# Attention and a 60-expert layer on one core: the last chunk's members by one-hot products

## The reference

```python
x = x + attn(layernorm(x))     # 16 query heads, 4 key/value heads of 16, RMS norm on q and k, RoPE, no mask
x = x + ffn(layernorm(x))

def ffn(x):
    shared = (silu(x @ Wg) * (x @ Wu)) @ Wd * sigmoid(x @ w_gate)      # 704 hidden
    probs = softmax(x @ gate_w.T)                                      # 60 experts
    weights, sel = top_k(probs, 4)
    for e in range(60):                                                # each 176 hidden
        acc += cw[:, e] * ((silu(x @ W1[e].T) * (x @ W3[e].T)) @ W2[e].T)
    return shared + acc
```

## Time and profile before

| | us |
|---|---|
| median of 3 runs | 790.94 |
| lowest, highest | 782.4, 792.96 |
| the profiled execution | 785.71 |
| its span, first to last instruction | 783.9 |
| PE busy in the span | 664.1 |
| DVE, ACT, POOL busy | 471.6, 513.3, 390.6 |

### The profile page before, as it was taken

The page is one execution under the profiler, slowest core; times in us unless marked ns, Lnnn a source line. Parts: engine busy times, 40 slices in busy tenths (PEclk is TensorE's granted clock), DMA queues, the critical chain, the costliest instruction groups (busy, mean ns, idle before and its releaser), DMA issues.

```text
span 783.9 us, 17631 instructions
## 1 busy us (share of the span) xinstructions
PE 664.1 (85%) x5559; PEld 333.9 (43%) x5559; DVE 471.6 (60%) x1290; ACT 513.3 (65%) x880; POOL 390.6 (50%) x356
## 2 busy tenths in 40 slices
PE   3578999999999989996979399999989898779900
PEld 1363333343433433455858287444434343334400
DVE  4782434336534454527583325999778797589645
ACT  1559778988898888862232112898778787768800
POOL 2134062164022265446052447788888888778700
PEclk9959999999999999999999699999999999889955
DMA  5000000000004000059100123366667586673178
GB/s 176 0 1 1 1 1 1 1 1 28 1 28 139 28 29 20 9 135 153 17 28 1 10 62 102 95 219 186 222 211 230 183 247 198 182 223 82 71 265 283
DMA packets 43293, 75.89 MB, mean 97 GB/s; under 512 B 8216, under 2 KB 24028, under 8 KB 43204
## 3 DMA queue, kind: packets, MB, share of 16 engines
q1 hardware_dynamic: 33316, 53.81, 23.1%
q0 software_dynamic: 9888, 20.98, 9.2%
HBM read 58.07 MB, written 16.68 MB: 95 GB/s over the span
## 4 chain that ended last, share of the span: by engine, by line
PE 55%; DMA 10%; DVE 9%; POOL 9%; issue 7%; ACT 6%; SPq 1%; ACTq 1%; DVEq 1%; POOLq 0%
PE p_o L1495 15%; PE p_s L1483 10%; PE p_gu L1651 5%; POOL expert_out L772 3%; DMA expert_out<-ys,goes_to 3%; PE p_y L1672 3%; POOL xs L752 3%; DMA members<-place,slot 2%; DMA fin<-expert_out 2%; POOL members L699 2%; ACT placed L791 2%; DMA xs<-x_rows,choice_i 2%; PE p_st L1435 2%; PE bench L1422 2%; PE p_xs L1641 1%
## 5 line engine op out<-in xcount | busy, mean ns | idle before, releaser
L850 ACT ACTIVATE probs<-p_s 128x1024 f32<-128x1024 f32 x256 | 242.4, 1037 | 38.9 <-PE p_s L1483 36.6
L791 ACT ACTIVATE placed<-ring 88x512 f32 x256 | 150.3, 626 | 16.6 <-PE p_d L1593 9.3
L1321 DVE COPY placed<-ring 128x704 f32 x316 | 153.9, 529 | 8.9 <-SPq L578 6.4
L1495 PE MATMUL p_o<-probs,vext 128*32 128x512 f32 x1024 | 136.1, 604 | 0.5 <-DVE enr L1047 0.5
L772 POOL DMA_INDIRECT expert_out<-ys,goes_to x79 | 123.2, 1559 | 26.0 <-issue 18.0
L699 POOL DMA_INDIRECT members<-place,slot x64 | 64.6, 1010 | 142.7 <-PE p_o L1495 100.0
L752 POOL DMA_INDIRECT xs<-x_rows,choice_i x79 | 112.3, 1422 | 39.7 <-issue 19.8
L1651 PE MATMUL p_gu<-placed,xsT 128*32 128x352 f32 x1264 | 114.4, 481 | 0.7 <-DVE placed L1321 0.2
L1483 PE MATMUL p_s<-qst,kst 64*128 64x512 f32 x512 | 95.1, 447 | 2.3 <-ACT probs L850 1.6
L1672 PE MATMUL p_y<-placed,hT 88*32 88x256 f32 x1264 | 85.0, 387 | 7.4 <-ACT hT L791 7.3
L1483 PEld LDWEIGHTS p_s<-qst,kst 64*128 64x128 f32 x512 | 39.0, 184 | 87.1 <-ACT probs L850 76.4
(11 more groups left out here) (237 smaller groups left out, 1047.9 us busy)
## 6 DMA issues: line engine op xcount, KB each, us to landing
ring<-in_w_dram SPq DMA_DIRECT2D x60, 352.0 KB
ring<-in_w_dram SPq DMA_DIRECT2D x60, 176.0 KB
fin<-expert_out SPq DMA_DIRECT2D x16, 512.0 KB, 6.5
x_rows<-rows SPq DMA_DIRECT2D x4, 520.0 KB, 3.6
out_dram<-xres SPq DMA_DIRECT2D x4, 512.0 KB, 6.1
x2T_kept<-xt SPq DMA_DIRECT2D x3, 512.0 KB, 2.9
x2r<-x2T_kept SPq DMA_DIRECT2D x3, 512.0 KB, 8.8
sup<-in_sup_dram SPq DMA_DIRECT2D x2, 704.0 KB, 6.3
```

What stands on the lines that cost most here:

```text
L791: return nc.scalar.activation(o, i_, ACT.Copy, **kw)
L850: nc.scalar.activation(probs[:, j % NPB, :], p_s[j % NSB][:, :], ACT.Exp, scale=SCALE)\
L1321: last = v.tensor_copy(placed13[:, i % N13, h, :], ring[:, bass.ds(ring_at(tile, h), W13)])
L1495: last = mm(p_o[32 * g_:32 * g_ + 32, :], vext[c // 2][:, kb, rr // 2 + KP * h, :], probs[:, (2 * u + half) % NPB, h * QC:(h + 1) * QC], s ...
```

## The change

The last chunk's tokens no longer go through the DRAM table. The scatters of chunks 0 to 2 stay.

- `totals` is cut in two. Its first half (number of blocks of each expert, where its blocks begin) now stands ahead of `rank`; its second, `blocks`, makes block numbers and slots. For this the sum of `mask` and the running total `macc` are made in `route2`, not in `rank`.
- For the last chunk `rank` adds the beginning of the expert's blocks times 32, so the slot is the position in the list of all tiles; shift and mask by 128 give tile and row of each choice (`at_f`).
- `hots` makes on DVE, for each of the 16 choices and groups, a one-hot row over the 79 tiles (`tile_hot`) and one over the 128 rows, times the token's number less `REAL` (`place_hot`). `late` multiplies them on PE, 16 fp32 products summed in one PSUM bank, and `join` adds the sum to `block_members` after its load.
- POOL loads `block_members` when `blocks_ready` and the 48 scatters of chunks 0 to 2 are there.
- The order `after` is new; `down` is two entries, one for each pair of groups; `members` stands 4 gate/ups earlier. `THIRD` is thereby 13, not 17, and the number of gathers ahead of the gate/ups is 40 - 3 x 11 = 7, then 3 behind each of 11 gate/ups, 40 in all.

```diff
+        at_i = low("at_i", [P, 2, TQ * TOPK], i32)
+        at_f = low("at_f", [P, 2, TQ * TOPK])
+        from_none = low("from_none", [P, TQ * TOPK])
...
+        HALF = TQ * TOPK // 2
+        tile_hot = [t.rearrange("p n i -> p (n i)")[:, 0:HALF * NTILE].rearrange("p (n i) -> p n i", i=NTILE)
+                    for t in (rows[:, 0:TQ, :], hot[:, :, :, :].rearrange("p t k e -> p (t k) e"))]
+        place_hot = [t[:, :, :].rearrange("p a c -> p (a c)").rearrange("p (n i) -> p n i", i=P) for t in (enr, enc)]
...
-                 ("gu", 1, 0), ("down", 0, 0),
-                 ("soft", C3, 0), ("gu", 1, 1), ("rank", C3, 0), ("rank2", C3, 0), ("gu", 1, 2), ("totals", 0, 0), ("gu", 1, 3),
-                 ("split", 2, 0), ("gu", 1, 4), ("tables", 0, 0), ("gu", 1, 5), ("gu", 2, 0), ("down", 1, 0),
-                 ("gu", 2, 1), ("gu", 2, 2), ("split", 3, 0), ("gu", 2, 3), ("gu", 2, 4), ("members", 0, 0),
-                 ("gu", 2, 5), ("gu", 3, 0), ("down", 2, 0)]
-        after += [("gu", 3, f) for f in range(1, NFS)] + [("down", 3, 0)]
+                 ("gu", 1, 0), ("soft", C3, 0), ("down", 0, 0), ("totals", 0, 0), ("rank", C3, 0), ("rank2", C3, 0),
+                 ("down", 0, 1), ("gu", 1, 1), ("blocks", 0, 0), ("gu", 1, 2), ("hots", 0, 0), ("gu", 1, 3),
+                 ("split", 2, 0), ("tables", 0, 0), ("gu", 1, 4), ("late", 0, 0), ("gu", 1, 5), ("gu", 2, 0),
+                 ("join", 0, 0), ("down", 1, 0), ("members", 0, 0), ("down", 1, 1), ("gu", 2, 1), ("gu", 2, 2),
+                 ("split", 3, 0), ("gu", 2, 3), ("gu", 2, 4), ("gu", 2, 5), ("gu", 3, 0), ("down", 2, 0),
+                 ("down", 2, 1)]
+        after += [("gu", 3, f) for f in range(1, NFS)] + [("down", 3, 0), ("down", 3, 1)]
...
-            scatter(3, 0, TQ * TOPK)
-
 
             pool.wait_ge(blocks_ready, 1)
-            pool.wait_ge(scattered, 16 * NT * TOPK)
+            pool.wait_ge(scattered, 16 * (NT - TQ) * TOPK)
...
-            gathered = 4
+            gathered = NXS - 3 * (NCH * NFS - THIRD)
...
-
-            def rank(n, c):
-                v.tensor_tensor(hot[:, :, :, :], hot[:, :, :, :],
-                                bench[:, 0:TQ * E].rearrange("p (t o e) -> p t o e", o=1, t=TQ)
-                                .to_broadcast([P, TQ, TOPK, E]), ALU.mult).then_inc(bench_read, 1)
+                dve.wait_ge(mask_ready, c + 1)
                 v.tensor_reduce(mask_sum[:, :], mask[:, :, :].bitcast(fp32).rearrange("p t e -> p e t"), X_AXIS,
                                 ALU.add).then_inc(mask_summed, 1)
                 dve.wait_ge(mask_summed, c + 1)
                 v.tensor_tensor(macc[:, 1 - c % 2, :], macc[:, c % 2, :].bitcast(fp32), mask_sum[:, :], ALU.add)\
                     .then_inc(macc_ready, 1)
...
+            def rank(n, c):
+                ranks = bench[:, 0:TQ * E].rearrange("p (t e) -> p t e", t=TQ)
+                if c == C3:
+
+                    v.scalar_tensor_tensor(out=lg_now[:, :, 0:E], in0=cnt[:, 3:4, :].to_broadcast([P, TQ, E]),
+                                           scalar=float(BLK), in1=ranks, op0=ALU.mult, op1=ALU.add)\
+                        .then_inc(bench_read, 1)
+                    dve.wait_ge(bench_read, n + 1)
+                    v.tensor_tensor(hot[:, :, :, :], hot[:, :, :, :],
+                                    lg_now[:, :, 0:E].unsqueeze(2).to_broadcast([P, TQ, TOPK, E]), ALU.mult)\
+                        .then_inc(ranked, 1)
+                    return
+                v.tensor_tensor(hot[:, :, :, :], hot[:, :, :, :],
+                                ranks.unsqueeze(2).to_broadcast([P, TQ, TOPK, E]), ALU.mult).then_inc(bench_read, 1)
+
...
+                if c == C3:
+                    count(v.tensor_copy(slot[:, at:at + TQ * TOPK], rank_now[:, :, :].rearrange("p t k -> p (t k)")))
+                    v.tensor_single_scalar(at_i[:, 0, :], slot[:, at:at + TQ * TOPK], P.bit_length() - 1,
+                                           ALU.logical_shift_right)
+                    v.tensor_scalar(from_none[:, :], place[:, at:at + TQ * TOPK], -float(REAL), None, ALU.add)
+                    count(v.tensor_single_scalar(at_i[:, 1, :], slot[:, at:at + TQ * TOPK], P - 1, ALU.bitwise_and))
+                    v.tensor_copy(at_f[:, :, :], at_i[:, :, :]).then_inc(at_ready, 1)
...
             def totals():
 
-                def of(n):
-                    return eid[:, n * PER:(n + 1) * PER]
-
-                block_no, passed, real, whose, begins, inside, row_, row_or_none, slots, two, four = map(of, range(11))
                 dve.wait_ge(totals_in_psum, 1)
-                for h in range(PER):
-                    v.tensor_scalar(block_no[:, h:h + 1], tile_i[:, 0:1], float(PER), float(h), ALU.mult, ALU.add)
                 v.memset(cnt[:, 1, :], 1.0)
                 count(v.tensor_scalar(cnt_i[:, 0, :], p_tab[0][:, 0:E], float(BLK - 1), None, ALU.add))
                 count(v.tensor_single_scalar(cnt_i[:, 1, :], cnt_i[:, 0, :], BLK.bit_length() - 1,
                                              ALU.logical_shift_right))
                 count(v.tensor_scalar(cnt[:, 0, :], cnt_i[:, 1, :], 1.0, None, ALU.max))
                 count(v.tensor_tensor_scan(cnt[:, 2, :], cnt[:, 1, :], cnt[:, 0, :], 0.0, ALU.mult, ALU.add))
-                v.tensor_tensor(cnt[:, 3, :], cnt[:, 2, :], cnt[:, 0, :], ALU.subtract)
+                count(v.tensor_tensor(cnt[:, 3, :], cnt[:, 2, :], cnt[:, 0, :], ALU.subtract))
+
+            def blocks():
+
+                def of(n):
+                    return eid[:, n * PER:(n + 1) * PER]
+
+                block_no, passed, real, whose, begins, inside, row_, row_or_none, slots, two, four = map(of, range(11))
+                for h in range(PER):
+                    last = v.tensor_scalar(block_no[:, h:h + 1], tile_i[:, 0:1], float(PER), float(h), ALU.mult, ALU.add)
+                count(last)
...
+            def hots():
+
+                dve.wait_ge(at_ready, 1)
+                dve.wait_ge(rows_stored[C3 - 1], 16)
+                for n, to in enumerate(tile_hot):
+                    v.tensor_tensor(to, iota[:, 0:NTILE].unsqueeze(1).to_broadcast([P, HALF, NTILE]),
+                                    at_f[:, 0, n * HALF:(n + 1) * HALF].unsqueeze(2).to_broadcast([P, HALF, NTILE]),
+                                    ALU.is_equal)
+                for n in range(TQ * TOPK):
+                    last = v.tensor_scalar(place_hot[n // HALF][:, n % HALF, :], iota[:, :], at_f[:, 1, n:n + 1],
+                                           from_none[:, n:n + 1], ALU.is_equal, ALU.mult)
+                last.then_inc(hots_ready, 1)
+
+            def join():
+                dve.wait_ge(members_loaded, 16 * PER)
+                dve.wait_ge(late_in_psum, 1)
+                whole = block_members[0:NTILE, :, :].rearrange("p h r -> p (h r)")
+                v.tensor_tensor(whole, whole, p_tab[1][0:NTILE, 0:P], ALU.add).then_inc(members_joined, 1)
...
-                elif kind == "down" and c < NCH - 1:
-                    for q in range(TQ):
+                elif kind == "down" and (c < NCH - 1 or f):
+                    for q in (2 * f, 2 * f + 1):
...
+                for q in range(2, TQ) if half else ():
+                    pe.wait_ge(shared_added, c * TQ + q - 1)
+                    for f in range(NFS):
+                        last = part(q, f)
+                    last.then_inc(sdown_in_psum, 1)
+                if half:
+                    return
...
+                elif kind == "late":
+                    pe.wait_ge(hots_ready, 1)
+                    pe.wait_ge(bench_read, NJOBS)
+                    for n in range(TQ * TOPK):
+                        last = mm(p_tab[1][0:NTILE, 0:P], tile_hot[n // HALF][:, n % HALF, :],
+                                  place_hot[n // HALF][:, n % HALF, :], start=(n == 0), stop=(n == TQ * TOPK - 1))
+                    last.then_inc(late_in_psum, 1)
                 elif kind == "members":
-                    pe.wait_ge(bench_read, NJOBS)
-                    pe.wait_ge(members_loaded, 16 * PER)
-                    tr(p_tab[1][:, 0:NTILE], block_members[0:NTILE, :, :].rearrange("p h r -> p (h r)"),
+                    pe.wait_ge(members_joined, 1)
+                    pe.wait_ge(tables_ready, 1)
+                    tr(p_tab[0][:, 0:NTILE], block_members[0:NTILE, :, :].rearrange("p h r -> p (h r)"),
                        ident[0:NTILE, 0:NTILE]).then_inc(members_in_psum, 1)
```

More of the change, by code:

```diff
@@ L100, in attention_moe_block @@
         ones = keep("ones", [P, P], f32r)
-        iota_e = keep("iota_e", [P, E])
-        iota_i = keep("iota_i", [P, E], i32)
+        iota = keep("iota", [P, P])
+        iota_i = keep("iota_i", [P, P], i32)
         iota_k = keep("iota_k", [P, TOPK])
@@ L353, in attention_moe_block @@
         rank_ready = sem("rank_ready")
+        ranked = sem("ranked")
         exp_in = sem("exp_in")
@@ L360, in attention_moe_block @@
         totals_in_psum = sem("totals_in_psum")
```

(44 more changed lines are left out.)

18 lines of the change are left out of this document (7 added, 11 removed).

## The result

| | before | changed |
|---|---|---|
| median | 790.94 us | 767.26 us |
| lowest, highest | 782.4, 792.96 | 764.2, 769.28 |
| the profiled execution | 785.71 | 764.2 |
| its span | 783.9 | 762.4 |
| first product of the expert stage | 490.34 | 483.96 |

The ratio is 0.972, 95% interval 0.964 to 0.980: faster, by 23.7 us. Run again in a later group the same two kernels gave 0.985 (0.979 to 0.990), 13.1 us; the experiments come back to this. Of the 21.5 us between the two profiled executions, 6.4 lie ahead of the expert stage and 15.1 in it and its tail.

What follows compares the result with a forecast made beforehand. PE was taken to wait at a 15.4 us standstill and, in the expert stage, on POOL's issue. 785.7 - 11.4 - 12.7 = 761.6; with half of the 5.2 up to the median given back, 764 us, range 748 to 779.

Steps and rivals of the forecast that it cites:

- the stop: Around 440 to 445 us PE, DVE and ACT all stand; claimed to cost 15.4 us in all, slow clock included.
- The walk: Step-by-step timing of the new order from `mask` to ("gu",2,1) at 427.6 us, giving -11.4 us for the shared stage.
- the new steps cost PE 4.0: Shared stage: ("gu",2,1) starts at 427.6 instead of 423.60, so the added work takes 4.0 us of the 15.4 removed.
- The port: At 402 to 407 us, `hots` on DVE locks POOL out: each load 1.24 us later, 5 us in all, sum unchanged.
- The line through two points of the earlier trace: Expert stage: a tile takes (k + 2.03)/1.18 us for k POOL operations; 0.85 us an operation, -12.7 us for 15.
- the waiting for rows: Expert stage: the 9.5 us of waiting for gathered rows were expected gone, counted within the -12.7 us.
- (a): Expert stage bound by transfers, not POOL's issue, so gathers moved ahead gain nothing: 777 us; chance 0.15.
- (c): Expert stage: every gather moved ahead is worth POOL's full period: 748 us; chance 0.10.
- (b): Shared stage: new DVE steps eat the gain from the removed standstill, by clock and late members: 775 us; chance 0.12.
- (d): Three gaps within 10 us leave PE at 1.2 GHz for the rest of the shared stage: 830 us; chance 0.04.
- a gap over 3 us: Sign: no PE gap of more than 3 us was to appear between 400 and 480 us.
- above the 5: Sign: `late` on PE was to take 3.5 to 5 us.

Runs made afterwards that it cites:

- the run in portions: Changed kernel with `hots` and `late` cut into parts with gate/ups between them: 764.16 us beside 765.86 of the changed kernel, ratio to the kernel before 0.981.

## Why the prediction was right, and where it was not

The time was 767.26 for 764.0, inside the range, and the profiled execution took 764.2 for 761.6. The mechanism was the one forecast: the stop is gone, and gathers moved ahead make the expert stage shorter. That the sum is so near is partly luck: the shared stage gave 5.0 us too little and the expert stage 2.4 too much. Point by point:

- **The stop is gone**, as said: the loads waited for the block numbers alone (401.74; predicted 401.8), `join` waited for nothing, and 440 to 445 us is full. The walk was right up to there within about 1 us: ("gu",1,1) started at 392.22 (391.1), `blocks` ended at 401.44 (400.8) and ("gu",1,4) started at 402.68 (402.2). The 1.1 us is a slow clock that the walk had not: behind a gap of 0.74 us at 383.09 and the short rank products, PE's granted clock was 0.55 over 385.7 to 389.5 us.
- **The shared stage gave 6.4 us and not 11.4**: the first `p_xs` started at 483.96, predicted 478.9. Two terms of "the new steps cost PE 4.0" were too small. `hots` ended at 410.6 instead of 407.5: its TENSOR_SCALAR took 0.42 us on the mean, not the 0.24 taken, and above the end of 0.345 that I had for it. Without POOL's loads it is 0.27, so the nearest rows were nearly right for the instruction and blind to what ran beside it. And `late` took 6.45 us for 4.5: 0.40 us a product, because 3.35 us of gap (2.7 predicted) left it at half clock for most of its length; the fast price, 0.22, was right. Together 3.1 + 2.0 = 5.1 us, which is all that was missing.
- **The port.** I had POOL's loads pay 5 us for `hots`, by the rule of the Trainium skill ("SBUF — State Buffer", section "Who interferes with whom"). The section says that whichever of the two issues first holds the shared ports and the other blocks, so by it either side can pay; I took one direction. The traces show the other: POOL's four loads are 0.2 us longer in all, and DVE's 16 instructions 2.4 us. That they disturb each other agrees with the page; that the ports are the cause is not shown by a run.
- **The 40 gathers** went out by 481.19, before the first product at 483.96. Predicted was before 479; both moved by the same late members. Most were 1.26 us apart, but the mean was 1.35, so they took 3 us more than 40 x 1.26.
- **The expert stage gave 15.1 us** (to the end of the span) for 12.7: 2.96 us a tile for 2.99. The line through two points of the earlier trace rows foretold the stages of 118, 133 and 148 operations within 2.5 us of the measured. At full DVE it was off: 14 operations in 30 us, not 12, so its slope is not to be trusted beyond this range. Nor does it hold tile by tile: in the new order with 25 or 40 ahead the first 20 take 2.63 to 2.72 us each, and the operations are paid for behind them. That the waiting for rows would go was wrong: it is 8.6 us in one piece, where 9.5 were in three, and POOL's queue is still behind there.
- **The rivals.** (a) and (c) fell by the runs with 25 and 10 ahead. (b) named the right places, the clock and `hots`, and was half of what happened; only the better expert stage kept the sum. (d) fell: after 3.35 us of gap the clock was back by 417.4. I had called a gap over 3 us a sign against me, and by 0.35 us it was there; so was `late` with 6.45 us, above the 5.
- **What the sum did not know** is the group. With the kernel before at 779 us the changed one gives 13.1 us (0.985), at 832 us 9.4 (0.988), at 791 us 23.7. The changed kernel itself was 767.3 and 765.9 in two groups; the kernel before varies more. So the forecast time is confirmed twice, but the forecast gain, 26.9 us, is nearly met once and only half met in the repeat. The parts, by ratio: gathers alone 0.994, the new shared stage alone (25 ahead) 0.998 (0.992 to 1.004), so it is not told from nothing, both 0.985. Multiplied the two parts give 0.992, which the intervals don't separate from 0.985. That the shared stage's gain is partly lost in the expert stage fits the run in portions, but was not shown for this kernel.

## What to carry to other kernels

Where one queue has hardly a gap over most of a stage, the stage can be moved by the number of operations in it: move them ahead, and price each by a line through stretches of different load, not by the full period and not by nothing. A gain ahead of such a stage can be lost in it. Repeat the pair in another group before calling the gain a number. And when a short product chain follows a wait, price it at half clock, or put other work of the engine into the gap.

## What the runs showed of the hardware

- DVE's TENSOR_SCALAR of 128 fp32 elements with two column operands: 0.27 us alone, 0.375 to 0.46 beside POOL's issue of indirect loads. The loads took 1.90 to 1.94 us each with no TENSOR_SCALAR of `hots` beside them and 1.90 to 2.10 beside (2.33 once, in the kernel with portions).
- An fp32 product of 128 columns on one-hot rows is recorded as two MATMUL: 0.22 us at a granted clock of 1.0, 0.44 at 0.5.
- The same program took 4 to 7% longer in two groups (825 and 832 us for the kernel before, against 779 to 791), with engines stopping for 3 to 12 us with no releaser in the trace. With 40 gathers ahead POOL then waited 64 to 70 us for ACT in the expert stage, so its queue did not bound it.
